# Taking the identity products out of TensorE's queue between the last routing steps of a decoder layer with a routed feed-forward

## What is computed

```python
def _L0_ffn_ref(x, centroids, gamma, beta, W1, b1, W2, b2):
    def _sublayer(xs, g, b, W1e, b1e, W2e, b2e):
        mu = jnp.mean(xs, axis=-1, keepdims=True)
        var = jnp.mean(jnp.square(xs - mu), axis=-1, keepdims=True)
        h = (xs - mu) * jax.lax.rsqrt(var + EPS) * g + b
        return xs + jax.nn.relu(h @ W1e.T + b1e) @ W2e.T + b2e
    feats = x.reshape(-1, x.shape[-1])
    scores = jax.lax.stop_gradient(feats @ centroids.T)
    expert = jnp.argmax(scores, axis=1)
    alpha = jax.nn.sigmoid(jnp.sum(feats * centroids[expert], axis=-1, keepdims=True))
    ys = jax.vmap(_sublayer, in_axes=(None, 0, 0, 0, 0, 0, 0))(feats, gamma, beta, W1, b1, W2, b2)
    y = jnp.einsum('te,etd->td', onehot, ys)
    return (alpha * y + (1.0 - alpha) * feats).reshape(x.shape)
...
x = _layernorm(x + _L0_attn_ref(x, ...), axis=-1)
x = _layernorm(x + _L0_xattn_ref(x, ctx_1024, ...), axis=-1)   # cross, self, feed-forward
x = _layernorm(x + _L0_ffn_ref(x, ...), axis=-1)
```

## Time and profile before

| | us |
|---|---|
| median of 3 runs | 395.38 |
| lowest, highest | 394.95, 396.18 |
| the profiled execution | 394.81 |
| its span, first to last instruction | 393.1 |
| TensorE busy, share of the span | 97% |
| VectorE, ScalarE, GpSimd | 69%, 60%, 33% |
| mean granted clock of TensorE | 0.993 of full |

### The profile page before, as it was taken

How to read it: one execution, slowest core, us unless ns; L and a number is a source line. 1 busy time by engine, 2 the same in 40 slices (tenths; PEclk the granted TensorE clock), 3 DMA queues, 4 the chain that set the end, 5 groups by cost and what they waited for, 6 DMA issues and landing times.

```text
span 393.1 us, 10365 instructions
## 1 busy us (share of the span) xinstructions
PE 381.1 (97%) x3688; PEld 325.1 (83%) x3688; DVE 270.0 (69%) x931; ACT 237.0 (60%) x809; POOL 130.9 (33%) x258
## 2 busy tenths in 40 slices
PE   8999999999999999999999999999999999999992
PEld 8786788888888878888888898898988888999671
DVE  5478787878787786695886844788789777334431
ACT  1116967888787888999999986576513132332230
POOL 5152115133223042032322221444355536742331
PEclk9999999999999999999999999999999999999997
DMA  8953260162002010600000000892196423599200
GB/s 206 291 142 136 56 192 3 48 226 56 6 2 57 3 42 17 251 5 20 2 2 3 3 3 1 338 427 93 48 397 248 145 63 90 184 399 429 99 15 33
DMA packets 11831, 46.93 MB, mean 119 GB/s; under 512 B 1600, under 2 KB 6432, under 8 KB 9616
## 3 DMA queue, kind: packets, MB, share of 16 engines
q1 hardware_dynamic: 9712, 33.61, 25.3%
q0 software_dynamic: 1920, 12.35, 8.1%
q10 hardware_dynamic: 144, 0.26, 0.3%
HBM read 41.31 MB, written 4.91 MB: 118 GB/s over the span
## 4 chain that ended last, share of the span: by engine, by line
PE 94%; DVE 2%; POOL 1%; issue 1%; DVEq 0%; POOLq 0%
PE bank_pt L657 15%; PE bank_out L496 13%; PE bank_scores L511 7%; PE bank_out L522 7%; PE bank_scores L641 7%; PE bank_out L679 7%; PE bank_out L702 6%; PE bank_pt L692 6%; PE bank_out L482 5%; PE bank_out L489 5%; PE bank_out L551 3%; PE bank_scores L647 2%; PE bank_out L503 1%; PE bank_scores L741 1%; PE bank_out L593 1%
## 5 line engine op out<-in xcount | busy, mean ns | idle before, releaser
L1253 ACT ACTIVATE arena<-arena,negmaxc 112x375 f32<-112x375 f32 x128 | 77.1, 606 | 14.2 <-DVE negmaxc L1003 13.9
L1273 ACT ACTIVATE arena<-bank_pt 125x448 f32<-125x448 f32 (+1 forms) x128 | 65.1, 544 | 15.7 <-PE bank_pt L657 12.1
L1003 DVE CUSTOM_DVE_ANT_0 arena<-bank_scores,arena 112x375 f32<-112x375 f32 x128 | 65.5, 541 | 12.6 <-PE bank_scores L647 10.9
L657 PE MATMUL bank_pt<-ident,arena 112*125 112x112 f32 (+1 forms) x512 | 70.1, 271 | 0.0
L657 PEld LDWEIGHTS bank_pt<-ident,arena 112*125 112x125 f32 (+1 forms) x512 | 62.8, 175 | 8.2 <-issue 1.4
L496 PE MATMUL bank_out<-arena 128*112 128x256 f32 (+1 forms) x224 | 56.8, 383 | 0.0
L1364 POOL TENSOR_TENSOR vareps<-meanvar,scal 112x1 f32<-112x1 f32 (+1 forms) x49 | 10.3, 211 | 112.6 <-DVE meanvar L874 102.8
L1264 ACT ACTIVATE arena<-bank_scores,negmaxs 112x112 f32<-112x112 f32 x128 | 43.6, 356 | 6.4 <-DVE negmaxs L1009 2.8
L496 PEld LDWEIGHTS bank_out<-arena 128*112 128x112 f32 (+1 forms) x224 | 37.3, 182 | 7.0 <-issue 1.6
L1309 ACT ACTIVATE arena<-bank_scores,consts 128x128 f32<-128x128 f32 x64 | 18.2, 368 | 39.8 <-PE bank_scores L511 39.8
L511 PE MATMUL bank_scores<-arena 128*128 128x128 f32 x256 | 30.4, 276 | 1.0 <-DVE arena L1173 0.9
(11 more groups left out here) (190 smaller groups left out, 675.4 us busy)
## 6 DMA issues: line engine op xcount, KB each, us to landing
arena<-moe SPq DMA_DIRECT2D x8, 2048.0 KB, 13.1
arena<-ctxT SPq DMA_DIRECT2D x8, 375.0 KB, 3.9
arena<-mask SPq DMA_DIRECT2D x8, 164.1 KB, 3.6
x_slots<-arena SPq DMA_DIRECT2D x8, 130.0 KB, 3.2
arena<-x_slots SPq DMA_DIRECT2D x8, 130.0 KB, 2.2
arena<-weights SPq DMA_DIRECT2D x2, 512.0 KB, 7.1
arena<-weights SPq DMA_DIRECT2D x1, 1024.0 KB, 5.2
arena<-fi SPq DMA_DIRECT2D x1, 1024.0 KB, 7.3
```

Source lines behind the costliest of these rows:

```text
L657: last = nc.tensor.transpose(dst[0:kp, j * S:(j + 1) * S], probs[0:S, (n % 2) * HG + j, c * kp:(c + 1) * kp], ident[0:S, 0:S])
L1003: v.tensor_tensor_reduce(out=probsC[0:S, i % (2 * HG)], in0=score_bank[j][0:S, 0:KX], in1=masks[0:S, u % 2], scale=-1.0, scalar=3.0e38, op ...
L1253: a.activation(probsC[0:S, i % (2 * HG)], probsC[0:S, i % (2 * HG)], ACT.Exp, bias=negmax["c"][0:S, u, at:at + 1], scale=-1.0, accum_out=s ...
L1273: a.activation(probsT[0:kp, n % RT, c], pt_bank[PT[stage, i] % RP][0:kp, 0:HG * S], ACT.Copy).then_inc(pt_free, 1)
```

## The change

The constant `WARM`, the five `wm` steps and the code for them are taken out. The order of all other steps stays as it was.

```diff
-WARM = 4
 WARM_FIRST = 6
 ORDER = (
...
-    "room rk f1 zb zn zx f2 sc zf wm*3 al wm en zx rk zb sc zn wm ei rk first*2 tot first*3 al first*3 ")
+    "room rk f1 zb zn zx f2 sc zf al en zx rk zb sc zn ei rk first*2 tot first*3 al first*3 ")
...
                     first_layer(0, (i,))
-                elif stage == "wm":
-                    if i == 0:
-                        pe.wait_ge(probs_ready, PROBS["sm", GROUPS - 1] + HG)
-                    for n in range(WARM):
-                        mm(bank[0][:, 0:128], ident[:, :], ident[:, :], start=True, stop=True)
```

## The result

The changed kernel took 397.56 us at the median (396.81 to 398.82, 22 executions), the kernel before 395.66 us in the same rounds (394.84 to 398.79, 22 executions). The ratio is 1.0044 (95% interval 1.0028 to 1.006): slower by 1.9 us, where 1.7 was forecast. The profiled execution took 397.83 us with a span of 396.1, against 394.81 and 393.1 before: 3.0 us more.

The account below looks back on a forecast made before the run. VectorE was taken to pace the stretch before the first expert, then TensorE to the end. Terms -0.1 + 0.9 + 0.95 gave +1.75, say +1.7 us, moving the median from 395.38 to 397.1 us; range 395.4 to 398.2.

Parts of the forecast that it names:

- The hole and the fall of the clock: TensorE idle 3.4 us, 309.66 to 313.06, waiting for VectorE; clock falls to 1.2 GHz between 311.7 and about 314.5; chance 0.57.
- Latency: Slower small steps from `zx` to the ranks of batch 7 delay `first` by 0.9 us, between 0.4 and 1.0.
- the gain at `ei`: Without the products ahead of it `ei` goes 0.8 us earlier, but `first` gains only 0.1 us, between 0 and 0.3.
- First tile at half rate: Low clock during `first` costs 0.95 us, the middle between 0 and 1.9 (back after 3.8 us of steady work).
- The other sum of the prediction: If transposes do not count as busy, `zx` and `ei` do not help the clock back: +2.7 us in total.
- The length of hole that the clock survives: The idle 3.4 us before `zx` exceed the 2.1 us after which the clock fell at the program's end, so it falls.
- The fifth step: Four identity products between the scores of batch 7 and `ei`, 1.14 us; removing them was to save 0.1 us.
- The base: The kernel before: median of three runs 395.38 us, clock at 9 of 10 or more everywhere between the two ends.
- The other way into tile 1: Last scatter, tile load and normalisation slip 0.9 us to 325.4, hidden behind TensorE's end of tile 0 at 326.5.
- The early return: Clock falls but is back before `first`, the small steps sufficing: +0.5 us, 395.9 us; chance 0.26.
- did the clock hold: Clock does not fall in the idle stretch from 309.66 to 313.06; 0.1 to 0.3 us saved, 395.2 us; chance 0.12.
- low past tile 0: Clock stays low until 325.4, waits at 321.3 and 325 interrupting the steady work: +4.5 us, 399.9 us; chance 0.05.

Follow-up runs that it names:

- the narrow products: Kernel before with the 16 identity products between scores of batch 6 and transposes of batch 7 streaming 8 columns, not 128: ratio 1.0116.
- the kernel without the four steps: Kernel before without the four steps of identity products between scores of batch 6 and transposes of batch 7: ratio 1.0072, median 398.88 us.
- the kernels with more fill there: Kernel before, last product step moved behind `ei`, four or two products added before scores of batch 7: ratios 1.0006 (0.9992 again) and 0.9992.
- the one with half the fill: Kernel before with 8 identity products in place of 16 between scores of batch 6 and transposes of batch 7: ratio 1.0023.

## Why the prediction was right, and where its steps were off

- *The hole and the fall of the clock: right.* VectorE made the same hole (`zx` at 313.3 behind `zf` at 312.8), and the clock fell at 313.1. All 22 executions of the changed kernel are at 396.81 us or more.
- *Latency, +0.9 us: too much; measured 0.30 with the gain at `ei` in it.* The step that failed is the ranks of batch 6, "0.9 later", of which "0.5 remains". I had given each further pass 0.12 us from identity passes that stream 128 columns. The ranks stream 8, and the rows show their four passes and the two of `zx` done by 314.53 (L716, 314.01 + 0.52), 0.36 later than before (313.49 + 0.34) once the 0.34 of the start is off; VectorE took them at 314.60, when its copy had ended (314.22 + 0.38), so nothing of it remained; nor did the 0.1 at `zx`. The one-hot rows of batch 7 start 3.79 us after its `zf` starts, against 3.73 before, where 0.5 more was forecast. The ranks of batch 7 did cost what was said: 0.54 + 0.37 against 0.36 + 0.20 is 0.35 for the 0.4.
- *First tile at half rate, +0.95 us (0 to 1.9): too little; measured 2.38.* The step that failed is the upper bound: 3.8 us of steady work, taken from the start of the program. The low level lasted until 323.4, 5.6 us after `first` began. By the chains, the first 8 passes took 1.91 us for 1.13, `tot` 0.23 for 0.34 (before, it waited for VectorE's slots), the other 24 passes 4.50 for 2.78. In the kernel that lacks only the fifth step it came back 3.3 us into `first`. Taking the middle on the ground that the small steps "are more than an idle engine" made the term smaller still; the narrow products suggest that such passes didn't help. What sets how long the level stays low is open.
- The two errors were of opposite sign: 0.9 - 0.1 + 0.95 = 1.75 expected, 2.7 in the profiled execution. That the medians moved by 1.9 where 1.7 was forecast is partly luck, here and in the base. The other sum of the prediction, 0.9 + 1.9 - 0.1 = 2.7 for transposes that do not count, meets the 2.7 by accident: neither of its terms is met.
- *The length of hole that the clock survives: right by a narrow margin.* The prediction set 3.4 us against the 2.1 us after which the clock fell at the end of the one trace. In the other twelve profiles here it fell 2.1 to 5.3 us after the last product, so the one trace had given the shortest of these times, and by them a hole of 3.4 us does not make the fall sure. In the changed kernel the clock fell 3.1 us after the scores of batch 6 (310.0), before `zx` began; in the kernel without the four steps only at 314.5, when `zx` and ranks were under way.
- *The fifth step: wrong in the prediction.* I costed its removal as a gain of 0.1 us. Taken out alone it costs 1.0 us by the ratio (1.4 between the medians of its rounds, which lie in different clusters), and with the other four gone it is a burden of 1.1 to 1.3 us.
- *The base: not seen.* I took the kernel before for one that never loses its clock. A third of its executions lie in the upper cluster; in the rounds of the result it is 8 of 22, which lifts the median from 395.36 us (the other 14) to 395.66. The three runs that I had, 394.95 to 396.18 us, all lie below the upper cluster and could not show it. Of the 1.1 us by which the profiled pair lies further apart than the medians (3.0, 1.9) this is 0.3; 0.55 more is that the profiled execution of the kernel before lies below that 395.36, and 0.27 that the profiled one of the changed kernel lies above its own median.
- *The other way into tile 1: right, with more room than forecast.* The load was late too (normalisation of tile 1 at 324.52, against 323.95), and TensorE's end of tile 0 at 327.87 covered it, some 3 us later where the forecast had 1.1 (326.5, 325.4).
- *The rivals.* The early return did not occur in the profiled execution, nor did the clock hold. The case "low past tile 0" did not occur: it was back one microsecond before the second layer.

What is not settled: how many microseconds each execution of the changed kernel was low. 17 of the 22 have a mean clock of 0.981 or 0.982, the other five 0.985 to 0.989, and the times of those five (397.37 to 397.54) lie among the others'; the low stretch at the end of the program, of unequal length, is in all of these means. Nor is it known why the clock held for 5.3 us of idleness at the end of one trace and for 2.1 in another. Nor was a profile taken of an execution of the kernel before in its upper cluster; that the clock falls there behind the sparse steps is inferred: from the mean clocks of nine of them, from the kernel without the fifth step, whose profile shows it, and from the kernels with more fill there, which have no upper cluster. No kernel had the sparse stretch filled and the hole left open, so what the hole needs by itself is not known.

## What to carry to other kernels

Products that nobody reads can be a step that the path needs: before taking them out, find what the engine would do in their place and whether the stretch behind it is sparse as well. Count cover over the whole thin stretch and with products of full width, and put it where the engine waits in any case, behind the steps that others wait for; a part of it in the wrong place can cost more than none. And where the clock can fall by chance, compare the executions one by one with their mean clock, since the median of a kernel with two clusters says little.

## What the runs showed of the hardware that I had not expected

TensorE passes that stream 8 columns kept the engine busy for 3.50 of 3.50 us by the profile, and the granted clock fell from 2.4 to 1.2 GHz all the same, at 314.7 us; float32 transposes over 128 columns in the same place kept it at 1.00 in both profiled executions until the hole was over, and in one of them throughout. After the fall the low level lasted 10.2 us in the changed kernel, in the one without the four steps and in that with narrow products, 6.8 us in the one with half the fill and in that with transposes and no fifth step, and 3.4 us in the kernel that lacks only the fifth step, though `first` was equally dense in all. At the end of the program the clock fell 2.1 us after the last product in one trace and 5.3 us after it in another.
